# Self-attention stage of a decoder layer: value products moved behind the first projection of each slot, and ScalarE's copy of that projection moved ahead of the reciprocal

## The reference, cut to what matters

```python
q, k, v = split((layernorm(x) @ w_qkv.T))            # 16 heads of 32
s = (q @ k.T) / sqrt(32) - abs(t - s_pos) * slope_h  # masked to -10000 above the diagonal
num = 0.5 * (1 + s * rsqrt(1 + s * s))
out = (num @ v) / (num.sum(-1) + 1e-6)
x = x + out @ w_out.T
# then: cross-attention over 750 context tokens, then a top-2 mixture of 8 experts
```

## Time and profile before

| what | value |
|---|---|
| median of three executions | 3276.03 us |
| the profiled execution, its own time | 3286.76 us |
| its span | 3284.9 us |
| TensorE busy over the span | 3043.6 us (93%) |
| first stage, 44 to 771 us: TensorE busy | 629.95 of 727.00 us, granted clock 0.92 |
| second stage, 771 to 1966 us: TensorE busy | 1103.77 of 1195.00 us, granted clock 0.96 |
| third stage, 1966 us to the end: TensorE busy | 1290.29 of 1318.90 us, granted clock 0.99 |
| passes 3 to 5 of the first stage | 84.35, 84.34 and 84.30 us |

### The profile page before, as it was taken

How to read it: one execution, slowest core, us unless ns; L and a number is a source line. 1 busy time by engine, 2 the same in 40 slices (tenths; PEclk the granted TensorE clock), 3 DMA queues, 4 the chain that set the end, 5 groups by cost and what they waited for, 6 DMA issues and landing times. The chain is left out here.

```text
span 3284.9 us, 50660 instructions
## 1 busy us (share of the span) xinstructions
PE 3043.6 (93%) x19312; PEld 2491.3 (76%) x19312; DVE 1644.6 (50%) x3785; ACT 1347.1 (41%) x2298; POOL 733.1 (22%) x560
## 2 busy tenths in 40 slices
PE   6889999878999999999999959999999999999997
PEld 4667777756777777777777738888888888888886
DVE  5888888863555556555555633323233323333321
ACT  5677777764555555555555521111111111121111
POOL 0000000011112122221212124242524242424232
PEclk9889999989999999999999969999999999999999
DMA  2011111124111111111111013141414141414132
GB/s 98 23 35 46 44 37 42 45 80 132 39 38 38 44 37 51 54 37 37 38 43 37 17 48 102 52 97 52 97 52 104 51 102 52 97 52 97 52 74 36
DMA packets 93874, 189.70 MB, mean 58 GB/s; under 512 B 17568, under 2 KB 27552, under 8 KB 91712
## 3 DMA queue, kind: packets, MB, share of 16 engines
q1 hardware_dynamic: 79168, 158.68, 15.9%
q0 software_dynamic: 14592, 29.43, 5.0%
HBM read 140.25 MB, written 47.82 MB: 57 GB/s over the span
## 5 line engine op out<-in xcount | busy, mean ns | idle before, releaser
L1757 ACT ACTIVATE f_hf<-f_h 128x448 f32<-128x448 f32 x256 | 139.8, 546 | 1012.4 <-PE f_h L1784 979.7
L1728 DVE CAST f_hh<-f_hf 128x448 fp32r<-128x448 f32 x256 | 106.4, 416 | 845.3 <-ACT f_hf L1757 824.5
L1799 PE MATMUL f_y<-f_w2h,f_hh 128*128 128x512 f32 x896 | 357.4, 399 | 0.0
L1687 POOL TENSOR_TENSOR f_w1l<-f_raw,f_w1h 128x512 fp32r<-128x512 f32 x128 | 182.4, 1425 | 777.3 <-DVE f_w1h L1711 777.1
L1799 PE MATMUL f_y<-f_w2h,f_hl 128*128 128x512 f32 x896 | 354.0, 395 | 0.0
L1799 PE MATMUL f_y<-f_w2l,f_hh 128*128 128x512 f32 x896 | 352.2, 393 | 0.0
L1380 ACT ACTIVATE c_s_sb<-c_s_sb,c_nmx 112x750 f32<-112x750 f32 x256 | 236.1, 922 | 200.4 <-DVE c_nmx L1214 198.5
L1372 ACT COPY c_pT<-psum 125x672 f32<-125x672 f32 x256 | 184.8, 722 | 244.8 <-PE psum L1475 236.8
L1475 PEld LDWEIGHTS psum<-a_ident,c_s_sb 112*125 112x125 f32 x1536 | 199.2, 195 | 93.7 <-issue 88.8
L1784 PE MATMUL f_h<-f_xTh,f_w1h 128*128 128x448 f32 x1024 | 254.8, 370 | 2.9 <-DVE f_xTl L1716 1.4
L1784 PE MATMUL f_h<-f_xTl,f_w1h 128*128 128x448 f32 x1024 | 250.0, 366 | 0.0
(11 more groups left out here) (246 smaller groups left out, 5833.5 us busy)
## 6 DMA issues: line engine op xcount, KB each, us to landing
f_raw<-in_w SPq DMA_DIRECT2D x128, 512.0 KB, 4.2
h_craw<-in_ctxT SPq DMA_DIRECT2D x16, 1125.0 KB, 5.1
a_x_in<-in_x SPq DMA_DIRECT2D x9, 896.0 KB, 5.7
a_xr<-in_x SPq DMA_DIRECT2D x8, 896.0 KB, 6.0
x_dram<-a_xr SPq DMA_DIRECT2D x8, 896.0 KB, 4.8
q_dram<-a_q SPq DMA_DIRECT2D x32, 224.0 KB, 5.6
h_q<-q_dram SPq DMA_DIRECT2D x16, 448.0 KB, 5.4
c_x<-x_dram SPq DMA_DIRECT2D x16, 448.0 KB, 4.9
```

Of the source, the lines that this page charges most:

```text
L1687: pool.tensor_tensor(w1s[1][:, l % NSLOT].rearrange("p k c -> p (k c)"), raw1[:, g % 2, l % 2, :], w1s[0][:, l % NSLOT].rearrange("p k c - ...
L1728: dve.tensor_copy(hs[0][:, l % 2, c * HC:c * HC + HC], hf[:, c, :]).then_inc(h_hi, 1)
L1757: act.activation(hf[:, c, :], H[:, 0:HC], ACT.Gelu_apprx_tanh).then_inc(free, 1)
L1799: mm = pe.matmul(Y[t][:], hs[a][:, l % 2, 128 * t:128 * t + 128], w2s[b][:, l % NSLOT, :], start=j == 0 and q == 0, stop=last_of_expert(l) ...
```

## The change

Two groups of lines trade places, and nothing else differs. On TensorE `values(i, s)` comes behind the units of the slot's first half. On ScalarE the copies of these units come ahead of the reciprocal. No instruction is added or taken away, except for register bookkeeping.

```diff
--- before.py
+++ after.py
@@ -699,9 +699,9 @@
                     root_of(0, i + 1)
                 if s == 1 and kind != "first":
                     root_of(1, i - 1)
-                reciprocal(i, s)
                 for unit in units(kind, s, 0):
                     evacuate(i, kind, unit)
+                reciprocal(i, s)
                 late = units(kind, s, 1)
                 for unit in late[:1]:
                     evacuate(i, kind, unit)
@@ -860,11 +860,11 @@
                     made(i, kind, "Q0", "K0")
                 if has_step(kind, s + 1):
                     scores(*step(i, s + 1))
+                for unit in units(kind, s, 0):
+                    run(i, kind, unit)
                 if s == 4:
                     made(i, kind, "V2", "V3")
                 values(i, s)
-                for unit in units(kind, s, 0):
-                    run(i, kind, unit)
                 if kind == "first" and s == 4:
                     pe.wait_ge(w_lo, KC + len(pieces))
                 for unit in units(kind, s, 1):
```

## The result

Seven executions of each kernel on the same chip: the changed kernel 3293.17 us in the median (3288.80 to 3296.99), the kernel before 3275.17 us (3261.45 to 3278.54). The ratio on record is 1.0064, with a 95% interval of 1.0050 to 1.0078, so the change costs 16 to 26 us; the two medians lie 18 us apart. The forecast was +23 us, 3299.

A forecast was written before the change was run, and what follows sets the result against it. Some first-stage slots were taken as bound by TensorE's work, others by a 9.92 us ScalarE-VectorE loop. Gates +8.3 us and clock +14.8 us gave +23, or 3299 us; own range 3287 to 3306, overall 3281 to 3311.

The forecast's parts named there:

- K3's gate: Slot 1: K3 waits for OUT2's bank, freed by VectorE, so V2 ends later: +1.13 us a pass.
- Q0's gate: Slot 5: Q0 waits for the low part of T1c3 on VectorE, TensorE idle 4.4 us: +0.53 us a pass.
- Slots 2 to 4: Units fill TensorE's waits, but VectorE's 9.92 us loop still bounds: no gain unless the lead reaches slot 5.
- The clock: Slot 5: the pause ahead of Q0 lowers TensorE's clock, 2.35 us in each of seven passes, +14.8 us net.
- the sum of 3304: Total if each of seven passes pays 3.1 us, half of a 6.27 us throttled stretch, 22 us in all.
- Pass 0's gain: Slot 1 of pass 0: K3 runs in the value products' 3.52 us wait, gaining 2.0 us, between 1.5 and 3.5.
- No order inside a slot makes smaller: Slots 5, 6, 7, 0 and 1 are bound by TensorE's sum of work, which reordering cannot reduce.
- ScalarE: 0: Copies ahead of the reciprocal cost nearly nothing; tightest in slot 3, done 0.2 us before VectorE needs it: 0 us.
- The lead is lost: TensorE reaches slot 5 some 3.7 us early, but waiting for Q0's operand uses up the lead altogether.
- Rival C: Lead kept, heavy slots shrink from 10.40 towards 9.92 us; 1.4 to 5.0 us a pass, 3255 us; chance 0.06.
- B: Only the gates cost, the pause ahead of Q0 lowers the clock in few or no passes: about 3283 us; chance 0.13.
- E: Clock stays low longer, a second stretch of 3.1 us in each pass: 3315 us; chance 0.07.

The follow-up runs named there:

- e6: Changed kernel with TensorE's part undone, only ScalarE's copies ahead of the reciprocal: 3273.27 us, ratio 1.0002 against the kernel before.
- e7: Changed kernel with ScalarE's part undone, only TensorE's new order kept: 3294.42 us, ratio 1.0071 against the kernel before.
- e9: Changed kernel with 16 extra matmuls ahead of Q0 and slot 1 in its old order in passes 1 to 7: 3288.63 us, ratio 1.0030.
- e3: Changed kernel with 16 extra matmuls filling the pause ahead of Q0 in slot 5: 3285.73 us, ratio 1.0041 against the kernel before.
- e8: Changed kernel with OUT1 ahead of slot 5's value products, its residual in slot 4, Q0 behind, slot 1 and transposes in old order: 3262.27 us, ratio 0.9969.
- e2: Changed kernel with slot 1 back in its old order in passes 1 to 7: 3291.46 us, ratio 1.0058 against the kernel before.
- e1: Changed kernel with slot 5 back in its old order on both engines: 3292.78 us, ratio 1.0055 against the kernel before.
- e5: Changed kernel with the new order in slots 2, 3 and 4 only: 3284.23 us, ratio 1.0035 against the kernel before.
- e10: e8 with slot 5 in its old order, OUT1 last in it and its residual where it was: 3288.47 us, ratio 1.0030 against the kernel before.

## Why the prediction was right, and where it was off

The direction, the mechanism and the places held, and +23 us lies inside the measured 16 to 26. That the sum came so near is partly luck, for several terms were off, in opposite directions.

| term | forecast | measured |
|---|---|---|
| pass 0 | -1.5 + 2.35 = +0.85 | -1.87 |
| pass 1 | 1.0 + 2.35 = +3.35 | +3.32 |
| pass 2 | 1.66 + 2.35 - 1.6 = +2.4 | +2.49 |
| passes 3 to 6, each | 1.66 + 2.35 = +4.0 | +3.97, +4.59, +4.65, +3.17 |
| pass 7 to the end of the stage | +0.5 | -0.9 |
| sum | +23 | +19.4 |

The measured column is the difference of one pair of profiles. The other pair (e6 and e7) gives 25.6, so the sum is good to some 5 us. Pass 6 shows only +3.17 since the kernel before had a fall in slot 4 there (10.67 us). The -0.9 at the end is no gain: that stretch took 125.06 us before and 123.44 in e6, in the same order.

- **K3's gate.** Forecast 1.13 us a pass; slot 1 grew by 1.17, and e9 gets 1.1 back. The wait itself is smaller than forecast: K3 starts 1.16 us behind the scores' last group (412.55 for 411.39), where the value products started 0.39 behind it (403.57 for 403.18), so 0.77. Another 0.19 is the order, in which "the same sum" takes 6.79 us for 6.60. The size was in part luck.
- **Q0's gate.** Forecast 0.53 us; with the clock held (e3) slot 5 is 0.59 longer, 0.44 of it the wait. Its pause was forecast at 4.4 us in all seven passes and was 3.71 to 4.23 in passes 2 to 6, 2.72 in pass 1 and 1.74 in pass 0.
- **Slots 2 to 4.** Forecast no gain, and there was none: slots 3 and 4 stayed at 9.92 us, and slot 2 grew by 0.2.
- **The clock.** Forecast 2.35 us in all seven passes; e3 gives 1.6 to 2.2, and the clock fell in six passes, not in pass 0. Together some 5 us too high. The upper bound took over the 6.27 us stretch of the earlier trace rows. The stretches here were shorter: an estimate from the windows is 5.0 us at the lower clock in slot 5 of pass 4 (mean 0.81 over 13.16 us) and 3.5 in pass 3 (0.86 over 12.62). Half of that is 2.5 and 1.8 us, and 2.17 and 1.63 over e3's 10.99 were measured. By the Trainium skill's rule in the page TensorE: Matmul & The Clock Gate, section on HAM oscillation, a loop with a long enough pause is throttled anew each round and pays half of the throttled time. From pass 1 on the trace agrees with both; the sum of 3304 was further off because its length of stretch came from another place.
- **Pass 0's gain.** Forecast 2.0 between 1.5 and 3.5; slot 1 fell from 13.00 to 9.92, so 3.1 (2.5 against e6's 12.47). K3 took the place of the wait (62.64 to 66.23, its first group at the lower clock, 1.86 us), and the value products started at 66.23, almost the same time as before (66.21 in the earlier trace rows). What I left out is that they then ran at the full clock, 1.28 us to V2 in place of 2.40 to K3. V3 started at 70.97 in place of 75.09.
- **"No order inside a slot makes smaller."** This step failed. The sum of TensorE's work does depend on the order: 0.2 us more in slots 2, 6 and 7, some 4 us over the stage that no term had. It happened to offset most of the oversized clock.
- **ScalarE: 0.** Right (e6: 1.0002).
- **The lead is lost.** Right for the changed order: slot 6 stayed above 10.40. Rival C, a lead that is kept, fell; but its mechanism is real. e8 keeps one and gains 1.36 us a pass, just below the 1.4 from which C's price began: slots 5, 6 and 7 give 1.5, slot 2 is 0.14 longer (10.88 for 10.74), and slots 0 and 1 are as before.
- **Two slips in the range.** By its own terms the forecast's own range runs from 3276 + 17.6 - 5 = 3289, not 3287, to the 3304 that the prediction gives a little earlier, not 3306. Nothing hangs on them.

B (gates alone, 3283) fell with the clock of 0.81 to 0.86 in slot 5; what it describes only comes about when the pause is filled (e3). E (a second stretch at low clock) was not seen, for slot 6 had a clock of 1.00. Still open is when a pause lowers the clock and how long it then stays low: slot 5 of e2 took 0.4 us more than the changed kernel's in pass 4, at like pauses of 4.26 and 4.23 us.

## What to carry to other kernels

Removing an engine's wait in a stretch that another loop bounds only moved the wait here. So follow the lead to the next semaphore and read who is late there, and whether the stretch behind it is one that the engine bounds. If a pause must remain, put it where nothing is lost behind it, or move a ready piece of real work into it, so that the work is also gone from the crowded stretch (here the one edit turned +0.3% into -0.3%). And it may pay to keep matmuls of one shape and array use together: the extra 0.2 us, if the turn is its cause, sits in every iteration.

## What the runs showed that I had not expected

- The clock falls behind pauses well under 4.38 us, and the length of the last pause does not decide it alone. It fell behind 3.73 us in e1 and e5, 2.72 in pass 1 of the changed kernel, 2.22 in pass 0 of e2 (slot 5 of 12.21), 1.88 in pass 2 of the kernel before and 1.77 in pass 0 of e1. It stayed up behind 1.87 in pass 3 of the kernel before, 2.01 in pass 0 of e7 and 1.74 in pass 0 of the changed kernel; e2 and the changed kernel have the same order in pass 0. Each kernel has one profile here, so how often a pause of one length lowers the clock is not shown.
- The price depends on where the fall sets in and on how soon the clock is back: some 0.5 us less where it came within Q0's first group, and in e10 1.2 us less (11.96 for 13.13) where it came within the first value products. Adding matmuls that compute nothing shortened a pass by 2.1 us.
- Costs at gates and of the clock are not additive: 1.1 us a pass taken out upstream (e2) came back by about half in slot 5, and stayed when the pause was filled (e9).
- Value products behind full-array transposes start 0.17 us later than a product does there.
